# Rearranging the prologue of a one-core attention and expert kernel: load order, engine of the scalings and key copies, place of the statistics, order of the first maxima

## The chip, the cores and the metric

The kernel runs on one core of one Trainium2 chip. The metric is device microseconds of one execution; lower is better. Three runs of the kernel before gave 1066.01, 1066.62 and 1066.67 us, so its time is 1066.62 us. One further execution was profiled; all rows come from it.

## What is computed

One layer: cross attention, then a mixture of experts, both with residuals. Cut to what matters here:

```
l  = layernorm(layernorm(x))               # x: 2048 x 256, "latents"; gains ln_l_g, ln_l_b
c  = layernorm(ctx)                        # ctx: 1601 x 192, "context"; gains ln_x_g, ln_x_b
q  = l @ Wq.T
kv = concat([c @ Wkv.T, l @ Wlkv.T])       # 1601 + 2048 keys and values, 4 heads of 64
attn = softmax(where(mask, rmsnorm(q)*qn_g/8 @ (rmsnorm(k)*kn_g).T, -max))   # mask on the context keys
x  = x + (attn @ v) @ Wo.T + bo
x  = x + top2_of_8_experts(layernorm(x))   # silu(gate)*up, then w2
```

All matrices are float32. The change touches only what comes before the first attention score.

## The kernel before, in words

Each engine has its own instruction stream; semaphores order them. The program has a prologue (the first 140 us), 16 attention units (four query blocks by four heads), and the expert stage. The prologue is the subject.

**Tiles.** Keys lie in 29 tiles of 128: t = 0 to 12 are context (13 tiles, 192 channels), t = 13 to 28 are latents (16 tiles, 256 channels). The prologue is a software pipeline written by hand: in step s each engine runs its function `pro` with work on different tiles, in this order.

- TensorE (L1283): transposes of the normalised tile s into `bX` (L1288); after that the products of tile s-1 for queries and keys into `bA` (L1300), in latent steps the query transposes of an older tile (L1312), the values of tile s-1 into `bV` (L1317); last the four key transposes of tile s-3 into `bK` (L1328). The products of L1300 wait until `knat` of two tiles earlier has been read out of the same bank. L1328 waits until both readers of the previous `bK` are done (semaphores `s2`, `klo`).
- VectorE (L894): multiplies `bX` by the gain and adds the offset, giving `xT` (L902, two instructions); normalises tile s+1 into `xn` (L891); sums squares of tile s-2 (`ss`, L911); writes the low part of the keys of tile s-4 (L916, semaphore `klo`, below called the key rest); reciprocal norms (L923, L926); normalised queries `qn` (L932) and keys `knat` (L937) of tile s-2.
- ScalarE (L633): squares of tile s-2 (L640), the high part of the keys of tile s-4 into `S2` (L646), the values (L651), the scaled queries `QT` (L659), the norms (L665), and the copy of the high keys from `S2` into `S1` (L669).
- GpSimd: zeroes rows 64 to 127 of all of `S2` in one memset (L451), then per tile writes the mask column into `knat` (L459) and adds the output bias to x (L465), which SyncE stores.

**Head of the prologue.** SyncE loads context tiles 0-1, then 2-11, then the last, then x, the latent weights and others. The queue of ScalarE issues the context weights, eight loads of the gains, four of the query and key norm gains, and the mask, whose element (t, p) goes to partition p (L624), one byte per descriptor. VectorE takes the statistics of all 13 context tiles (L867 to L884), normalises tile 0, then waits for the mask (L943), the norm gains and the eight gains (L953), and only then runs step 0.

**x statistics.** After step 6 VectorE takes the statistics of all 16 x tiles in one go (L959 to L962).

**End of the prologue.** VectorE waits for everything, zeroes and fills the lower rows of `Q2` (L983, L984), and makes two small constants. ScalarE copies the first queries (L693, L697), TensorE computes 32 score pieces of 464 keys (`piece`, L1346, query tile by query tile) of which VectorE takes the maxima (L1002). These 32 must be done before the first unit. SyncE waits for all keys and queries (L351 to L353) before it loads the first pieces of expert weights, which ScalarE and GpSimd split (L735, L492); six of them stand in ScalarE's stream before the first unit.

Of the kernel before, what the change touches and what calls it, by code (L numbers as in the profile page):

```python
# [4 lines left out]
F32 = mybir.dt.float32  # L5
# [8 lines left out]
P = 128  # L14
# [9 lines left out]
QB = 4  # L24
# [74 lines left out]
def run_units(body):  # L99
    for b in range(NB):  # L100
        for h in range(H):
            body(Unit(b, h))

# [21 lines left out]
def build(nc, x, ctx_in, mask, ln_x_g, ln_x_b, ln_l_g, ln_l_b, qn_g, kn_g, w_lat, w_ctx, wo_t, bo,  # L125
# [13 lines left out]
    with stack:  # L139
# [122 lines left out]
        m_u8 = sb("m_u8", [P, NC], U8, at=t0)  # L262
# [59 lines left out]
        FIRST_BANKS = M_BANKS + [bS[i][:, k, :] for i in range(2) for k in range(2)]  # L322
# [8 lines left out]
        def _(sp):  # L331
            for n, (lo, hi) in enumerate(CTX_LOADS):
# [4 lines left out]
                .then_inc(sem("ctx_in_l"), 16)  # L337
            sp.dma_start(V[:, NC:NK, :], x.rearrange("(t p) d -> p t d", p=P)).then_inc(sem("x_in"), 16)
# [3 lines left out]
            sp.dma_start(rt[:], router_t.rearrange("(k p) n -> p k n", p=P)).then_inc(sem("c_rt"), 16)  # L342

# [90 lines left out]
        def _(pool):  # L434
# [4 lines left out]
            pool.memset(ident[:], 0.0).then_inc(sem("id0"), 1)  # L439
            pool.memset(ctxt[:, NC - 1, :], 0.0).then_inc(sem("ctx_pad"), 1)  # L440
            pool.memset(mcol[:], 0.0).then_inc(sem("mc0"), 1)
            pool.wait_ge(sem("id0"), 1)
            pool.affine_select(out=ident[:], in_=ident[:], compare_op=ALU.not_equal, fill=1.0, base=0,
                               pattern=[[-1, P]], channel_multiplier=1).then_inc(sem("ident"), 1)
            pool.memset(knat[:, :, :, D:D + 1], -1.0).then_inc(sem("kn0"), 1)

            pool.wait_ge(sem("ident"), 1)
            pool.wait_ge(sem("ctx_pad"), 1)
            pool.wait_ge(sem("mc0"), 1)
            pool.wait_ge(sem("kn0"), 1)  # L450
            pool.memset(S2[D:P, :, :].bitcast(F32), 0.0).then_inc(sem("s20"), 1)  # L451
            pool.wait_ge(sem("s20"), 1)


            def k_mask(t):
                if not (t.i is None and t.off < 2):
                    pool.wait_ge(sem("kT_mm"), t.v - 1)
                pool.wait_ge(sem("mcol"), 1)
                pool.tensor_copy(knat[:, t.par, :, D + 1], mcol[:, bass.ds(t.v, 1)].to_broadcast([P, H]))\  # L459
                    .then_inc(sem("kmask"), 1)  # L460
# [6 lines left out]
            pool.wait_ge(sem("c_bo"), 16)  # L467
            for t in range(NC + 2):
                k_mask(Step(None, t))
                if t == 3:  # L470
                    pool.wait_ge(sem("x_in"), 16)
                if t >= 3:
                    x_bias(t - 3)
            for t in range(NC - 1, NT):
                x_bias(t)
# [19 lines left out]
            def constants():  # L495
# [15 lines left out]
                pool.tensor_copy(row[:], row_i[:]).then_inc(sem("row"), 1)  # L511
                pool.wait_ge(sem("U"), 1)
# [4 lines left out]
                pool.wait_ge(sem("row"), 1)  # L517
# [93 lines left out]
        def _(act):  # L611
            act.dma_start(wc[0:P, 0, :], w_ctx[0:P, :]).then_inc(sem("wc_in"), 16)
            act.dma_start(wc[0:CIN - P, 1, :], w_ctx[P:CIN, :]).then_inc(sem("wc_in2"), 16)
            gains = ((ln_x_g, CIN), (ln_x_b, CIN), (ln_l_g, DIM), (ln_l_b, DIM))
            for n, (g, w) in enumerate(gains):
                for k in range(2):
                    r = min(P, w - k * P)
                    act.dma_start(cols[0:r, 2 * n + k:2 * n + k + 1],
                                  g[k * P:k * P + r].rearrange("(p a) -> p a", a=1)).then_inc(sem("cols"), 16)
            for n, g in enumerate((qn_g, kn_g)):  # L620
                for k in range(2):
                    act.dma_start(gcol[k * D:(k + 1) * D, n:n + 1], g.rearrange("(p a) -> p a", a=1))\
                        .then_inc(sem("gq"), 16)
            act.dma_start(m_u8[:, 0:NC - 1], mask[0:(NC - 1) * P].rearrange("(t p) -> p t", p=P),  # L624
                          allow_slow_non_contiguous=True).then_inc(sem("m_in"), 16)
            act.dma_start(m_u8[0:CTX - (NC - 1) * P, NC - 1:NC],
                          mask[(NC - 1) * P:CTX].rearrange("(p a) -> p a", a=1)).then_inc(sem("m_in"), 16)


            act.wait_ge(sem("bn"), NC)  # L630
            act.activation(sda[:, 0:NC], mvs[:, 0:NC, 1], ACT.Sqrt, bias=eps[:, 0:1]).then_inc(sem("sd_c"), 1)

            def pro(s, b, c, q=0):  # L633
# [8 lines left out]
                kT = bK[0:A, 0, :].rearrange("p (h c) -> p h c", h=H)  # L642
                if c:
                    c_ = s.back(4)
                    act.wait_ge(sem("kT_mm"), c_.v + 1)
                    act.copy(S2[0:A, :, bass.ds(c_.v * P, P)], kT).then_inc(sem("s2"), 1)  # L646
# [20 lines left out]
                if c:  # L667
                    act.wait_ge(sem("s2"), c_.v + 1)
                    act.copy(S1[0:D, :, bass.ds(c_.v * P, P)],  # L669
                             S2[0:D, :, bass.ds(c_.v * P, P)].bitcast(F32)).then_inc(sem("s1"), 1)  # L670

            def lat_sd():
                act.wait_ge(sem("bn"), NK)
                act.activation(sda[:, NC:NK], mvs[:, NC:NK, 1], ACT.Sqrt, bias=eps[:, 0:1]).then_inc(sem("sd_l"), 1)
                act.wait_ge(sem("v2"), 1)
                act.activation(sda[:, NC:NK], va[:, NC:NK], ACT.Sqrt, bias=eps[:, 0:1]).then_inc(sem("sd_l"), 1)

            act.wait_ge(sem("s20"), 1)
# [125 lines left out]

            for k in range(2):
                act.wait_ge(sem(f"xb_st{k}"), 16 * NT // 2)
            q_hi(0, 0, 0)
            q_hi_1(0, 0, 0)
# [46 lines left out]
        def _(dve):  # L855
# [10 lines left out]
            dve.memset(xT[CIN - P:P, :, 1, :], 0.0).then_inc(sem("xT0"), 1)  # L866
# [8 lines left out]

            for n, (lo, hi) in enumerate(CTX_LOADS):
                dve.wait_ge(sem(f"ctx_in{n}"), 16)
                for t in range(lo, hi):
                    stats(ctxt[:, t, :], t)
            dve.wait_ge(sem("ctx_in_l"), 16)  # L880
            stats(ctxt[:, NC - 1, :], NC - 1)
            aggregate(0, NC)
            dve.wait_ge(sem("sd_c"), 1)
            link(dve.reciprocal(rsd[:, 0:NC], sda[:, 0:NC]))  # L884
# [9 lines left out]
            def pro(s, a, ln, b, c):  # L894
                if a:
                    dve.wait_ge(sem("xT_mm"), s.v + 1)
                    if not (s.i is None and s.off < 2):
                        dve.wait_ge(sem("v_mm"), s.v - 1)
                    for k in range(2):
                        r = P if (k == 0 or a == 'l') else CIN - P  # L900
                        g0 = 0 if a == 'c' else 4
                        dve.tensor_scalar(xT[0:r, s.par, k, :], bX[s.par][0:r, 0, k * P:(k + 1) * P],  # L902
                                          cols[0:r, g0 + k:g0 + k + 1], cols[0:r, g0 + 2 + k:g0 + 3 + k],
                                          ALU.mult, ALU.add).then_inc(sem("xT"), 1)
# [36 lines left out]
            apply(Step(None, 0), 'c')  # L941

            dve.wait_ge(sem("m_in"), 32)  # L943
            dve.wait_ge(sem("mc0"), 1)
            NF = NC - 1
            link(dve.tensor_scalar(mcol[:, 0:NF], m_u8[:, 0:NF], -1.0, BIG, ALU.add, ALU.mult))
            link(dve.memset(mcol[:, NF:NC], -BIG))
            dve.tensor_scalar(mcol[0:CTX - NF * P, NF:NC], m_u8[0:CTX - NF * P, NF:NC], -1.0, BIG, ALU.add, ALU.mult)\
                .then_inc(sem("mcol"), 1)
            dve.wait_ge(sem("gq"), 64)  # L950
            dve.scalar_tensor_tensor(gT[:], gcol[:, 0:1], SCALE, gcol[:, 1:2], ALU.mult, ALU.mult)\
                .then_inc(sem("gs"), 1)
            dve.wait_ge(sem("cols"), 128)  # L953
            dve.wait_ge(sem("xT0"), 1)
            run_steps(dve, 0, 2, lambda s: pro(s, 'c', 'c', 0, 0))
            run_steps(dve, 2, 4, lambda s: pro(s, 'c', 'c', 'c', 0))
            run_steps(dve, 4, LAT_AT + 1, lambda s: pro(s, 'c', 'c', 'c', 1))

            dve.wait_ge(sem("x_in"), 16)  # L959
            for t in range(NT):  # L960
                stats(V[:, NC + t, :], NC + t)
            aggregate(NC, NK)  # L962
            run_steps(dve, LAT_AT + 1, LAT_AT + 2, lambda s: pro(s, 'c', 'c', 'c', 1))
            L = slice(NC, NK)
            dve.wait_ge(sem("sd_l"), 1)
            link(dve.reciprocal(rsd[:, L], sda[:, L]))
# [313 lines left out]
        def _(pe):  # L1280
# [65 lines left out]
            def piece(v, h, k, banks):  # L1346

                i, g = divmod(k, NG)
                if k == 0:
                    pe.wait_ge(sem("q2"), v + 1)  # L1350
# [305 lines left out]
```

## Time and profile before

| | |
|---|---|
| median of 3 runs | 1066.62 us |
| profiled execution | 1064.43 us |
| its span, first to last instruction | 1062.7 us |
| busy over the span | TensorE 91%, VectorE 67%, GpSimd 54%, ScalarE 46% |
| mean granted TensorE clock | 0.971 |

The chain that ended last is 70% TensorE and 7% VectorE of the span. In the page's 40 slices (26.6 us each) TensorE reads 2, 6, 9, 9, 8, 6 tenths in the first six and 9 nearly everywhere after; VectorE reads 3, 8, 8, 8, 8, 6 there. A row of the timeline gives start, duration, engine, line, operation, output and inputs, the count of merged instructions, and in brackets the idle time before it with what ended it.

### The profile page before, as it was taken

The page shows a single profiled execution, that of the slowest core. Times are in us where ns is not written, and L with a number is a line of the kernel's source. Part 1 is how long each engine was busy: PE and PEld are TensorE (multiplying, and loading weights), DVE is VectorE, ACT ScalarE, POOL GpSimd, SP SyncE. Part 2 cuts the span into 40 slices and gives each one's busy share as a digit, 9 for nine tenths or more (in the row PEclk, how much of TensorE's full clock was granted, in tenths as well). Part 3 has the DMA queues.
Part 4 walks back from the last instruction along what each step waited for, and adds up shares of the span by engine and source line. Part 5 has one row for each costly group of instructions (what it writes and reads, how often), then busy time and mean ns, then how long its engine had stood idle before and what let it go on. Part 6 is the DMA issues. An engine that isn't in the chain of part 4 may idle for free.

```text
span 1062.7 us, 15497 instructions
## 1 busy us (share of the span) xinstructions
PE 965.9 (91%) x4570; PEld 629.9 (59%) x4571; DVE 710.6 (67%) x1412; ACT 484.5 (46%) x752; POOL 570.1 (54%) x439
## 2 busy tenths in 40 slices
PE   2699869999999999999999999999996869999994
PEld 1565535556555556556656556565554658888883
DVE  3888886776786776776776776767787424444442
ACT  0456625545555455555555655654552213233231
POOL 5130016776677676776676676676700235565552
PEclk9899978999999999999999999999998889999998
DMA  6010021121122121221122121221338673333331
GB/s 185 20 46 15 0 94 54 52 74 60 60 67 68 65 74 61 74 71 60 65 80 65 60 85 55 70 75 60 131 142 338 235 295 52 53 52 52 53 51 24
DMA packets 70627, 87.51 MB, mean 82 GB/s; under 512 B 12619, under 2 KB 66828, under 8 KB 68524
## 3 DMA queue, kind: packets, MB, share of 16 engines
q1 hardware_dynamic: 52046, 70.73, 19.0%
q0 software_dynamic: 7488, 10.39, 6.0%
q10 hardware_dynamic: 11038, 5.71, 1.9%
q8 instruction: 28, 0.46, 0.2%
q14 instruction: 27, 0.22, 0.1%
HBM read 50.03 MB, written 36.77 MB: 82 GB/s over the span
## 4 chain that ended last, share of the span: by engine, by line
PE 70%; DVE 7%; issue 4%; DMA 3%; ACT 2%; ACTq 0%; POOL 0%; POOLq 0%; DVEq 0%
PE bPV L1433 20%; PE bM L1353 10%; PE bS L1422 9%; PE bS L1423 8%; DVE mpart L1002 2%; DMA out<-ysb,sidx 2%; PE bG L1543 2%; PE bY L1543 2%; PE bY L1544 2%; PE bY L1545 2%; PE bH L1560 2%; PE bT L1368 2%; ACT PT L780 2%; PE bG L1545 1%; PE bG L1544 1%
## 5 line engine op out<-in xcount | busy, mean ns | idle before, releaser
L1002 DVE TENSOR_REDUCE mpart<-bM 128x1 f32<-128x464 f32 x492 | 295.7, 635 | 126.5 <-PE bM L1353 125.1
L488 POOL TENSOR_TENSOR acc_p<-acc_p,PT 128x1024 f32<-128x1024 f32 x120 | 302.3, 2519 | 104.1 <-ACT PT L780 100.5
L780 ACT ACTIVATE PT<-bS 128x1024 f32<-128x1024 f32 (+1 forms) x240 | 237.6, 997 | 202.0 <-PE bS L1423 173.1
L1433 PE MATMUL bPV<-PT,V 128*64 128x512 f32 x928 | 230.6, 604 | 0.0
L1422 PE MATMUL bS<-QQ,S 128*128 128x512 f32 x464 | 189.8, 409 | 3.2 <-ACT PT L780 0.8
L1353 PE MATMUL bM<-S,QQ 128*128 128x464 f32 x492 | 174.2, 413 | 11.8 <-DVE mpart L1002 6.4
L1423 PE MATMUL bS<-QQ,S 128*128 128x512 f32 x464 | 183.7, 396 | 0.0
L1353 PEld LDWEIGHTS bM<-S,QQ 128*128 128x128 f32 x492 | 84.7, 191 | 95.1 <-DVE mpart L1002 70.3
L492 POOL TENSOR_TENSOR wraw<-wraw,whi 128x256 fp32r<-128x256 f32 x96 | 85.3, 889 | 69.3 <-ACT whi L735 69.3
L1433 PEld LDWEIGHTS bPV<-PT,V 128*64 128x64 f32 x928 | 58.7, 136 | 104.5 <-issue 91.8
L1422 PEld LDWEIGHTS bS<-QQ,S 128*128 128x128 f32 x464 | 87.8, 189 | 55.0 <-issue 26.0
L1423 PEld LDWEIGHTS bS<-QQ,S 128*128 128x128 f32 x464 | 87.9, 189 | 14.2
L1034 DVE TENSOR_TENSOR acc_d<-acc_d,PT 128x1024 f32<-128x1024 f32 (+1 forms) x58 | 89.0, 1535 | 0.8
L488 POOL TENSOR_TENSOR acc_p<-PT 128x1024 f32<-128x1024 f32 x15 | 38.3, 2556 | 86.5 <-ACT PT L780 86.5
L735 ACT CAST whi<-wraw 128x256 fp32r<-128x256 f32 x96 | 38.5, 402 | 78.9 <-DMA wraw<-w 78.5
L595 POOL DMA_INDIRECT out<-ysb,ring_s x34 | 54.3, 1597 | 37.0 <-POOL ring_s L588 30.4
L1254 DVE TENSOR_TENSOR hs<-hs,bU 128x512 f32<-128x512 f32 x39 | 26.8, 688 | 62.5 <-PE bU L1545 62.5
L836 ACT CAST hTe<-bH 128x512 fp32r<-128x512 f32 x39 | 22.9, 587 | 69.5 <-PE bH L1560 69.5
L1543 PE MATMUL bY<-W,hTe 128*128 x156 | 48.2, 309 | 1.5 <-DVE hTe L1248 1.5
L571 POOL DMA_INDIRECT xg<-xln_d,ring_g x34 | 34.4, 1012 | 27.0 <-POOL ring_g L567 27.0
L1544 PE MATMUL bY<-W,hTe 128*128 x156 | 45.0, 288 | 0.0
L1545 PE MATMUL bY<-W,hTe 128*128 x156 | 44.9, 288 | 0.0
(244 smaller groups left out, 1437.9 us busy)
## 6 DMA issues: line engine op xcount, KB each, us to landing
W<-wsp_d SPq DMA_DIRECT2D x16, 1536.0 KB, 11.7
wraw<-w SPq DMA_DIRECT2D x96, 128.0 KB, 2.4
wsp_d<-whi SPq DMA_DIRECT2D x96, 128.0 KB, 2.4
wsp_d<-wraw SPq DMA_DIRECT2D x96, 128.0 KB, 1.7
V<-x SPq DMA_DIRECT2D x1, 2048.0 KB, 12.6
xb_d<-xbs SPq DMA_DIRECT2D x16, 128.0 KB, 1.7
x<-xb_d ACTq DMA_DIRECT2D x12, 128.0 KB, 2.0
out<-x ACTq DMA_DIRECT2D x12, 128.0 KB, 1.7
```

Of the source, the lines that this page charges most:

```text
L488: pool.tensor_tensor(acc_p[:], one, PT[:, q % NPT, :, :], ALU.add).then_inc(sem("z_p"), 1)
L492: pool.tensor_tensor(wraw[:, n % 2, :].bitcast(F32R), wraw[:, n % 2, :], whi[:, n % 2, :].bitcast(F32), ALU.subtract).then_inc(sem("wsplit ...
L780: act.activation(PT[:, p % NPT, 0:n, :], bS[(w.h + p) % 2][:, 0:n, :], ACT.Exp).then_inc(sem("exp"), 1)
L1002: dve.tensor_reduce(mpart[:, i, g:g + 1], banks[k % len(banks)][:, 0:PIECE], AX, ALU.max)\
L1034: dve.tensor_tensor(acc_d[:, 0:m, :], one, PT[:, q % NPT, 0:m, :], ALU.add).then_inc(sem("z_d"), 1)
L1353: pe.matmul(banks[k % len(banks)][:, 0:PIECE], Q2[:, h % 2, i * P:(i + 1) * P], S2[:, h, g * PIECE:(g + 1) * PIECE], start=True, stop=True ...
L1422: pe.matmul(bS[sl][:, b, :], S1[:, h, c * P:(c + 1) * P], Q1[:, h % 2, :], start=True, stop=False)
L1423: last = pe.matmul(bS[sl][:, b, :], S2[:, h, c * P:(c + 1) * P], Q2[:, h % 2, :], start=False, stop=True)
L1433: last = pe.matmul(bPV[b * D:(b + 1) * D, 0, :], V[:, c, h * D:(h + 1) * D], PT[:, p % NPT, b, :], start=c < 2, stop=c >= NK - 2, skip_gro ...
L1543: pe.matmul(out_ap, st_hi, w[:, s, 0, lo:lo + n], start=first, stop=False)
L1544: pe.matmul(out_ap, st_lo, w[:, s, 0, lo:lo + n], start=False, stop=False)
L1545: return pe.matmul(out_ap, st_hi, w[:, s, 1, lo:lo + n], start=False, stop=last_)
```

## The change

- SyncE loads context tiles 0-3 first, then 4-11; the mask is loaded by rows (13 rows of 128 bytes) on SyncE's queue, in front of x; the latent gains and the query and key norm gains move to the end of SyncE's list of loads.
- GpSimd turns the mask into float, TensorE transposes it, VectorE makes the mask column from that.
- VectorE takes statistics of tiles 0-3 and starts; those of tiles 4-12 come after tiles 0 to 2 are normalised.
- The scalings (`xT`) run on ScalarE as Identity with scale and bias columns.
- The copy of the high keys into `S1` runs on GpSimd, which also zeroes `S2` by tile.
- The x statistics are spread over steps 4 to 8 (3, 3, 3, 3, 4), their aggregation is in step 9.
- `Q2`'s lower rows are set by GpSimd; ScalarE copies the first queries two steps earlier; the first 32 pieces go by age of the keys, and use the score banks first.

```diff
+def place(v, k):
+    return (k % QB, k // QB) if v == 0 else divmod(k, NG)
...
-        FIRST_BANKS = M_BANKS + [bS[i][:, k, :] for i in range(2) for k in range(2)]
+        FIRST_BANKS = [bS[i][:, k, :] for i in range(2) for k in range(2)] + M_BANKS
...
+            sp.wait_ge(sem("mc0"), 2)
+            sp.dma_start(m_u8[0:NC - 1, :], mask[0:(NC - 1) * P].rearrange("(t p) -> t p", p=P)).then_inc(sem("m_in"), 16)
...
-            pool.memset(S2[D:P, :, :].bitcast(F32), 0.0).then_inc(sem("s20"), 1)
+            def rest_zero(lo, hi):
+                pool.memset(S2[D:P, :, lo * P:hi * P].bitcast(F32), 0.0).then_inc(sem("s20"), 1)
+            def keys_hi(t):
+                pool.wait_ge(sem("s2"), t + 1)
+                pool.tensor_copy(S1[0:D, :, t * P:(t + 1) * P], S2[0:D, :, t * P:(t + 1) * P].bitcast(F32))\
+                    .then_inc(sem("s1"), 1)
...
+            rest_zero(0, 4)
+            pool.wait_ge(sem("m_in"), 32)
+            pool.tensor_copy(mrow[0:NC, :], m_u8[0:NC, :]).then_inc(sem("mcol"), 1)
+            for t in range(NK + 2):
+                if t < NC + 2:
+                    k_mask(t)
+                if t + 4 < NK:
+                    rest_zero(t + 4, t + 5)
+                if 3 <= t < 3 + NT:
+                    x_bias(t - 3)
+                if t >= 2:
+                    keys_hi(t - 2)
+            pool.wait_ge(sem("v_mm"), NK)
+            pool.memset(Q2[D:P, :, :].bitcast(F32), 0.0).then_inc(sem("q20"), 1)
+            pool.memset(Q2[D:D + 2, :, :].bitcast(F32), 1.0).then_inc(sem("q20"), 1)
...
             def pro(s, a, b, c, q=0):        # ScalarE
+                if a:
+                    act.wait_ge(sem("xT_mm"), s.v + 1)
+                    for k in range(2):
+                        act.activation(xT[0:r, s.par, k, :], bX[s.par][0:r, 0, k * P:(k + 1) * P], ACT.Identity,
+                                       scale=cols[0:r, g0 + k:g0 + k + 1], bias=cols[0:r, g0 + 2 + k:g0 + 3 + k])
                 if b:   # squares, as before
                 if c:   # S2, as before, and a wait for rest_zero
                 ...
-                if c:
-                    act.copy(S1[0:D, ...], S2[0:D, ...].bitcast(F32)).then_inc(sem("s1"), 1)
...
+            for t in range(4, NC - 1):       # VectorE
+                pro(Step(None, t), 'c', 'c', 1)
+                for _ in range(X_STATS.get(t, 0)):
+                    stats(V[:, NC + done, :], NC + done)
+                if t == X_AGGR_AT:
+                    aggregate(NC, NK)
...
+            pe.wait_ge(sem("mcol"), 1)
+            pe.transpose(bK[:, 0, 0:NC], mrow[0:NC, :], ident[0:NC, 0:NC]).then_inc(sem("mcol"), 1)
...
+            pe.wait_ge(sem("q20"), 2)
+            pe.wait_ge(sem("sq"), NK)
+            pe.wait_ge(sem("q_n"), NT)
+            pe.wait_ge(sem("knat"), NK)
+            for k in range(NM):
+                if k == len(FIRST_BANKS) - len(M_BANKS):
+                    pe.wait_ge(sem("v_cp"), NK)
+                    pe.wait_ge(sem("qT"), NT)
+                piece(0, 0, k, FIRST_BANKS)
...
-CTX_LOADS = ((0, 2), (2, NC - 1))
-LAT_AT = 6
+CTX_LOADS = ((0, 4), (4, NC - 1))
+X_STATS = {4: 3, 5: 3, 6: 3, 7: 3, 8: 4}
+X_AGGR_AT, X_SD_AT = 9, 10
```

## Rows read from the trace of the kernel before

**Rows 1.** Busy time in one stretch: PE, PEld, DVE, ACT, POOL, clock, DMA, GB/s.

```profile
39.40:48.80 9.40, 3.15 (x15) 2.33 (x15) 9.27 (x42) 1.78 (x5) 0.87 (x2) 0.82 0.04 14
```

**Rows 2.** Timeline of TensorE: the transposes of tiles 3, 13 and 28.

```profile
26.83 0.38 PE L1288 MATMUL bX<-ident,xn 128*128 128x128 f32 x2
...
65.77 0.38 PE L1288 MATMUL bX<-ident,xn 128*128 128x128 f32 x2
...
122.19 0.38 PE L1288 MATMUL bX<-ident,xn 128*128 128x128 f32 x2
```

**Rows 3.** Timeline of the first 22 us, all engines.

```profile
1.79 12.47 POOL L451 MEMSET S<- 64x14848 f32 x1
...
3.04 1.22 ACTq L618 DMA_DIRECT2D cols<-ln_x_b  x2
...
19.32 0.17 DVE L946 TENSOR_SCALAR mcol<-m_u 128x12 f32<-128x12 uint8 x1 [2.73 <-DMA m_u<-mask]
...
19.79 0.71 DVE L902 TENSOR_SCALAR xT<-bX,cols 128x128 f32<-128x128 f32 x2
...
21.39 1.91 PE L1300 MATMUL bA<-wc,xT 128*128 128x256 f32 x4
```

**Rows 4.** DMA issues by line, first 30 us: KB each, median us to landing.

```profile
cols<-ln_x_b ACTq DMA_DIRECT2D x1, 0.2 KB, 6.1
```

**Rows 5.** Timeline of one context step, from the transposes of tile 10.

```profile
56.35 0.38 PE L1288 MATMUL bX<-ident,xn 128*128 128x128 f32 x2
...
56.73 0.73 POOL L465 TENSOR_TENSOR xbs<-V,bob 128x256 f32<-128x256 f32 x1
...
56.86 0.72 DVE L902 TENSOR_SCALAR xT<-bX,cols 128x128 f32<-128x128 f32 x2 [0.22 <-PE bX L1288]
...
58.23 0.69 DVE L916 TENSOR_TENSOR S<-bK,S 64x512 f32 x1
...
59.07 0.60 PE L1328 MATMUL bK<-ident,knat 128*66 128x128 f32 x4 [0.32 <-DVE S L916]
...
59.56 0.43 PE L1288 MATMUL bX<-ident,xn 128*128 128x128 f32 x2
```

**Rows 6.** Timeline of one latent step, from the transposes of tile 22.

```profile
99.22 0.38 PE L1288 MATMUL bX<-ident,xn 128*128 128x128 f32 x2
...
100.69 0.69 DVE L911 TENSOR_REDUCE ss<-bSq 128x8 f32<-128x512 f32 x1
...
103.00 0.41 DVE L937 TENSOR_TENSOR knat<-bA,rn 128x256 f32<-128x256 f32 x1
...
103.56 1.95 PE L1300 MATMUL bA<-wl,xT 128*128 128x512 f32 x4 [0.37 <-DVE knat L937]
```

**Rows 7.** Groups by line and shape, first 160 us: busy us, mean ns, idle before.

```profile
L646 ACT CAST S<-bK 66x512 fp32r<-66x512 f32 x11 | 6.4, 581 | 5.3 <-PE bK L1328 5.3
...
L869 DVE BATCH_NORM_STATS2 st<-V 128x6 f32<-128x256 f32 x16 | 5.3, 409 | 0.0
...
L640 ACT ACTIVATE bSq<-bA 128x256 f32<-128x256 f32 x13 | 4.7, 364 | 7.5 <-PE bA L1300 7.5
...
L665 ACT ACTIVATE nrm<-ss 128x4 f32<-128x4 f32 x13 | 2.7, 205 | 17.4 <-DVE ss L911 17.4
...
L659 ACT ACTIVATE QT<-bV,gT 128x256 f32<-128x256 f32 x4 | 1.9, 474 | 0.0
...
L631 ACT ACTIVATE sda<-mvs,eps 128x13 f32<-128x13 f32 x1 | 0.3, 306 | 0.0
```

**Rows 8.** Timeline of the prologue's end, all engines.

```profile
133.79 0.58 ACT L646 CAST S<-bK 66x512 fp32r<-66x512 f32 x1 [0.62 <-PE bK L1328]
...
135.72 0.81 SPq L363 DMA_DIRECT2D wraw<-w  x2
...
139.01 1.11 PE L1353 MATMUL bM<-S,QQ 128*128 128x464 f32 x2 [5.03 <-ACT QQ L693]
...
140.11 1.17 DVE L1002 TENSOR_REDUCE mpart<-bM 128x1 f32<-128x464 f32 x2
```

More of the change, by code:

```diff
@@ L874, in aggregate, with spread @@
                     dve.bn_aggr(mvs[:, t, :], st6[:, t, :]).then_inc(sem("bn"), 1)
[L876 to L882, printed above, removed]
+            def spread(lo, hi):
+                link(dve.reciprocal(rsd[:, lo:hi], sda[:, lo:hi]))
+            lo, hi = CTX_LOADS[0]
+            dve.wait_ge(sem("ctx_in0"), 16)
+            for t in range(lo, hi):
+                stats(ctxt[:, t, :], t)
+            aggregate(lo, hi)
             dve.wait_ge(sem("sd_c"), 1)
-            link(dve.reciprocal(rsd[:, 0:NC], sda[:, 0:NC]))
+            spread(lo, hi)
             def apply(t, kind):
@@ L892, in apply, with pro @@
                                   ALU.subtract, ALU.mult).then_inc(sem("ln"), 1)
[L894 to L904, printed above, removed]
+            def pro(s, ln, b, c):
                 if ln:
@@ L941, in _ @@
             apply(Step(None, 0), 'c')
-            dve.wait_ge(sem("m_in"), 32)
-            dve.wait_ge(sem("mc0"), 1)
+            for t in range(2):
+                pro(Step(None, t), 'c', 0, 0)
+            dve.wait_ge(sem("ctx_in1"), 16)
+            dve.wait_ge(sem("ctx_in_l"), 16)
+            for t in range(hi, NC):
+                stats(ctxt[:, t, :], t)
+            aggregate(hi, NC)
+            dve.wait_ge(sem("sd_c"), 2)
+            spread(hi, NC)
+            pro(Step(None, 2), 'c', 'c', 0)
@@ L959, in _ @@
[L959 to L963, printed above, removed]
-            L = slice(NC, NK)
-            dve.wait_ge(sem("sd_l"), 1)
-            link(dve.reciprocal(rsd[:, L], sda[:, L]))
-            link(dve.tensor_tensor(va[:, L], rsd[:, L], rsd[:, L], ALU.mult))
-            dve.tensor_tensor(va[:, L], va[:, L], mvs[:, L, 1], ALU.mult).then_inc(sem("v2"), 1)
@@ L999, in piece @@
             def piece(v, k, banks):
-                i, g = divmod(k, NG)
+                i, g = place(v, k)
                 dve.wait_ge(sem("m_mm"), NM * v + k + 1)
@@ L1174, in _ @@
             maxima(0)
+            for q in range(2):
+                dve.tensor_copy(twin[q * D:(q + 1) * D, :], ident[q * D:(q + 1) * D, q * D:(q + 1) * D])\
+                    .then_inc(sem("twin"), 1)
+            dve.memset(onec[:], 1.0).then_inc(sem("twin"), 1)
             run_units(unit)
```

204 lines of the change are left out of this document (106 added, 98 removed).

## The prediction

> **What bounds the kernel now.** I read the chain of waits first: it is mostly TensorE from the first attention unit on, and nothing there is edited. So I looked at the stretch before it. The timeline of the first 22 us shows that VectorE stands until 19.32 us for the mask to land, although tile 0 has been normalised; the first scaling starts at 19.79 us and the first product at 21.39 us [rows 3]. From there I follow the pipeline by the transposes of each tile: tile 3 at 26.83, tile 13 at 65.77, tile 28 at 122.19 us [rows 2], so 38.94 us for ten context steps and 56.42 us for fifteen steps that end with the latents. The ten contain one hole: from 39.4 to 48.8 us TensorE is busy 3.15 of 9.40 us and VectorE 9.27, at a granted clock of 0.82 [rows 1]; that is the 16 x statistics in one go. Elsewhere a context step takes 59.56 - 56.35 = 3.21 us, and the row before its end says what held TensorE: the key rest on VectorE [rows 5]. The latent steps take (122.19 - 99.22)/6 = 3.83 us on average [rows 2, 6], and there the product of L1300 was held by `knat`, also on VectorE [rows 6]. The end runs from 122.19 to the first maximum at 140.11 us: 17.92 us [rows 2, 8].
>
> The sum is made in the profiled execution's time: span 1062.7 us, execution 1064.43 us, and the median of the runs is 1066.62 us, 2.2 us above. The edits lie in the first 140 us, so I take the difference off the median.
>
> **1. The head.** Gone from the path: the byte-wise mask, four of the eight gain loads, the norm gains, and the statistics of nine tiles. What ends last now? The statistics of four tiles can start when 384 KB have landed; I put that at 5 us, four statistics and aggregations at 1.5 us, the root, the reciprocal and tile 0 at 1.2 us: ready by 8 us, its transposes by 8.5. The two columns `ln_x_b` are issued at 3.04 to 4.26 us, so the last at about 3.7, and land 6.1 us after issue [rows 3, 4]: 9.8 us. These are issued at the same place in the new kernel, so I keep 9.8 (bounds: 8.5 if the slot is limited by the statistics; 13 if more traffic lies in front of them). ScalarE then scales tile 0 in 0.9 us, and the first product starts at 10.9 us instead of 21.39. TensorE's first products run slow, 1.91 us for four [rows 3], and will again. The mask's 13 rows follow the context loads on their queue; they are needed only by the key transposes of tile 0, some 8 us after the first product, so I cost the cast, the transpose and three small VectorE operations at nothing; if the rows landed after 18 us, each microsecond would show. Gain **10.4 us** (bounds 6.5 to 12).
>
> **2. One scaling on ScalarE.** No row has both a scale column and a bias column. Rows without a column: 364 ns for 256 elements, 205 ns for 4 [rows 7], so about 270 for 128. One column adds 100 to 110 ns: `QT` 474 against 364, `sda` 306 against 205 [rows 7]. So two columns give 270 + 210 = 480 ns; bounds 270 (nothing added) and 580. Consecutive ScalarE operations overlap by about 100 ns in this timeline, so a pair takes 0.76 us of the engine. VectorE's pair took 0.72 [rows 5]. The Trainium skill (ScalarE: Activation LUTs, "What ACT_TABLE_LOAD costs") has 186 ns + 0.833 ns per element, 93 ns more for each column operand and 93 ns of overlap; an estimate by it is 479 ns each and the same 0.76 us, which no row here shows for this form.
>
> **3. Context steps.** VectorE loses 0.72 us a step, ScalarE swaps the `S1` copy for a pair of scalings. But what counts is the chain that closes the loop on `bK`. New order on ScalarE: scalings, squares, `S2`. Hence from the transposes: 0.51 to the start of scaling [rows 5], 0.76 the pair, 0.27 the squares (364 less overlap), 0.58 `S2` [rows 7], 0.03, the key rest 0.69, 0.15 to the key transposes, 0.49 to the next transposes [rows 5]. Sum 3.48; where key transposes start back to back it is 0.04 less, so I use **3.45 us** against 3.21 (3.06 in the best steps). In the kernel before `S2` ran beside VectorE's scaling; now they are in series on one engine. Bounds: 3.03 with the cheap scaling, 3.65 with the dear one. VectorE has room for the statistics: 5.3 us / 16 = 0.33 each [rows 7], so 1.0 us in a step of which it uses 2.2 us of 3.45; for the step with four and for the aggregation I add 0.5 us in all. Ten steps: 34.5 + 0.5 = 35.0 against 38.94. Gain **3.9 us**. If the spread statistics weren't covered, it would be 6.5 us of VectorE work more, and the gain gone.
>
> **4. Latent steps.** Before: the sum of squares starts 1.47 us after the transposes (99.22 to 100.69), `knat` ends at 103.41, 4.19 after them, and the held product starts 0.15 later [rows 6]. The product of the next step can't start before 4.34, and from its start to the following transposes is a fixed piece c. Two steps take 4.34 + c = 7.66, so c = 3.32. After: the squares (0.58 for 512 elements, like `S2` [rows 7]) begin only behind the scalings, at 0.51 + 0.76 = 1.27, end at 1.85, and the sum starts at 1.88, 0.41 later than now; everything behind it on VectorE follows in the same order, so `knat` ends at 4.60. A step is (4.60 + 0.15 + 3.32)/2 = **4.03 us** against 3.83. Twelve of these, and 3.45 + 3.5 + 3.8 for the three in which latents enter: 59.1 against 56.42. Loss **2.7 us** (bounds: 0 with the cheap scaling; 4 with the dear one).
>
> **5. GpSimd.** Per step: mask column 0.2, a zeroing 12.47/29 = 0.43 [rows 3], bias 0.73 [rows 5], key copy of 512 elements. Its bounds: 0.43 (as a memset) and 1.46 (twice the bias add of 256 elements [rows 5]); I take 0.7, nearer the memset since it reads one tensor. With waits 2.4 us a step, at worst 3.2, both under 3.45, and nobody waits for `S1` before the end. So nothing in the steps.
>
> **6. The end.** ScalarE's two query copies (0.62 each) now stand in front of the last two `S2`, and the last products come 0.8 us later behind their transposes than before, as `knat` does. The last `S2`, which began 133.79 - 122.19 = 11.60 us after tile 28's transposes [rows 2, 8], begins at 12.7 and ends at 13.3. Then GpSimd: the last key copy, 14.05; only then, in its stream, the two memsets of `Q2`, 0.86 us each for 1024 elements (12.47 x 1024/14848 [rows 3]), 15.95. TensorE's first piece waits for them. It takes 0.55 (1.11 for two [rows 8]), and the first maximum starts at 16.6 us instead of 17.92. Gain **1.3 us** (bounds -0.5 with the dear copy, 4 if nothing held the memsets). The order by key age lets pieces start before the last keys, but the memsets come after the last `S2` anyway, so I give it nothing. The 32 maxima keep their pace on VectorE. The weight loads start 0.7 us later behind tile 28 than before (135.72 [rows 8]); with their six rounds they end shortly before the maxima.
>
> Sum: 10.4 + 3.9 - 2.7 + 1.3 = 12.9 us, so **1053.7 us**.
>
> **The rivals.** *A, the chain is as I say*: 1053.7. The `knat` and key-rest releasers speak for it; chance 0.57.
>
> *B, scaling is cheap* (about 0.29 us each, 0.4 less a pair, or overlapped with the squares): context steps 3.05, latent steps 3.83 as now; 10.4 + (38.94 - 31.0) + 0 + 1.3 = 19.6, so 1047.0. Against it: both column rows show an extra 100 ns. Chance 0.22.
>
> *C, the head opens late*: the gain columns or the mask rows land 4 us later than I think, because the larger first context load and the mask are in front of or beside them. 12.9 - 4.5: 1058. Chance 0.09.
>
> *D, given back at the end*: the weight split or the memsets on GpSimd hold the first unit 5 us or so. 1058 to 1060. Chance 0.07.
>
> *E, slower*: GpSimd's memset and copies (0.43 + 0.7, up to 1.9 us a step that weren't there) stretch VectorE's key rest and `knat` or block them. It decides from 12.9/25 = 0.5 us a step; at 0.7 us it costs 17.5, so 1071. Against it: VectorE's pair of 0.72 us ran right under a GpSimd add of 0.73 us [rows 5] and was no longer than elsewhere. Chance 0.03. The Trainium skill (GPSIMD Engine Reference, "Key points") says that GpSimd shares its SBUF interfaces with VectorE and names contention with VectorE operations that have two SBUF inputs or run in a two-port mode; the trace has no GpSimd copy in the prologue to test that with, and the key rest has one PSUM input.
>
> *F, no change* (the steps lengthen by all that the head wins): 0.02.
>
> **How the numbers follow.** A measurement of this kernel tells 0.2% (2.1 us) from no change. Faster: A, B, C and nearly all of D, 0.93; within: 0.03; slower: 0.04. The range 1045 to 1060.5 covers A with its bounds, B, C and most of D.
>
> **What would show it.** First product at about 11 us; scalings on ScalarE of 480 ns; context steps of 3.45 us held by the key rest, no hole near 40 us and the clock at 1.00 there; latent steps of 4.0 us held by `knat`; first piece held by GpSimd's `Q2` memset; first maximum near 126.6 us. Wrong: steps of 3.1 us (B), a wait for a DMA before 15 us (C), TensorE idle in front of the first unit behind the weight split (D), key rest above 0.9 us (E).

## The result and the profile after

Four runs of the changed kernel gave 1052.95 to 1056.56 us, median 1053.64 us, against 1066.32 us for the kernel before in the same comparison: ratio 0.9886, 95% interval 0.9867 to 0.9905. The same kernel in a later comparison (e0_changed, below) gave 1054.57 us, ratio 0.9887, interval 0.9871 to 0.9903. The profiled execution took 1052.95 us, its span 1051.1 us, 11.6 us less than before.

Read the span by the same marks as before. First the timeline of the head of the changed kernel, all engines.

```profile
5.08 1.14 DVE L912 BATCH_NORM_STATS2 st<-ctxt 128x6 f32<-128x192 f32 x4 [3.23 <-DMA ctxt<-ctx_in]
...
7.60 1.23 PE L1325 MATMUL bX<-ident,xn 128*128 128x128 f32 x4 [7.60 <-DVE xn L935]
...
9.30 0.28 POOL L494 CAST mrow<-m_u 13x128 f32<-13x128 uint8 x1 [5.56 <-DMA m_u<-mask]
...
10.47 1.49 ACT L672 ACTIVATE xT<-bX,cols 128x128 f32<-128x128 f32 x4 [3.65 <-DMA cols<-ln_x_b]
...
11.32 2.07 PE L1337 MATMUL bA<-wc,xT 128*128 128x256 f32 x4 [2.50 <-ACT xT L672]
```

Tiles 0 and 1 are transposed at 7.6 us and the mask is there at 9.3; ScalarE stands 3.65 us for the last gain load. The first product starts at 11.32 us, at 21.39 before [rows 3]. Next TensorE's timeline of the changed kernel, the transposes of tiles 3, 13 and 28.

```profile
16.81 0.44 PE L1325 MATMUL bX<-ident,xn 128*128 128x128 f32 x2
...
51.92 0.38 PE L1325 MATMUL bX<-ident,xn 128*128 128x128 f32 x2
...
111.25 0.38 PE L1325 MATMUL bX<-ident,xn 128*128 128x128 f32 x2
```

| | before | after | gain, us | predicted |
|---|---|---|---|---|
| to tile 3 | 26.83 | 16.81 | 10.0 | 10.4 |
| tile 3 to 13 | 38.94 | 35.11 | 3.8 | 3.9 |
| tile 13 to 28 | 56.42 | 59.33 | -2.9 | -2.7 |
| tile 28 to first maximum | 17.92 | 17.11 | 0.8 | 1.3 |
| sum | 140.11 | 128.36 | 11.75 | 12.9 |

Behind the first maximum both profiles take the same time within 0.2 us: 1062.7 - 140.11 = 922.6 and 1051.1 - 128.36 = 922.7. The medians differ by 12.7 us, the two profiled executions by 11.5.

The hole near 40 us [rows 1] is gone. Busy time and clock of the changed kernel in the stretch from tile 3 to 13 (columns as in rows 1):

```profile
16.80:51.90 35.10, 27.66 (x141) 20.16 (x141) 30.91 (x103) 20.03 (x61) 19.13 (x39) 1.00 0.11 33
```

The granted clock is 1.00, the upper of its two levels (2.4 GHz); VectorE is still busy 31 of 35 us, and not only with what I had thought. Groups of the changed kernel by line and shape, first 150 us:

```profile
L672 ACT ACTIVATE xT<-bX,cols 128x128 f32<-128x128 f32 x45 | 18.8, 454 | 44.6 <-PE bX L1325 41.0 <-DMA cols<-ln_x_b 3.6
...
L485 POOL CAST S<-S 64x512 fp32r<-64x512 f32 x29 | 17.5, 603 | 46.3 <-ACT S L687 46.2
...
L945 DVE TENSOR_REDUCE ss<-bSq 128x8 f32<-128x512 f32 x16 | 11.0, 690 | 12.2 <-ACT bSq L681 12.2
...
L935 DVE TENSOR_SCALAR xn<-ctxt,mvs,rsd 128x192 f32<-128x192 f32 x13 | 7.0, 549 | 0.6 <-PE bX L1325 0.6
```

A scaling takes 454 ns with its two columns, where 480 was worked out. VectorE now waits 12.2 us in all for the squares of latent tiles: that is the series of ScalarE. And `xn` takes 549 ns on average, 366 before, though nothing about it was edited. The timeline of one context step with statistics shows where.

```profile
26.97 0.38 PE L1325 MATMUL bX<-ident,xn 128*128 128x128 f32 x2
27.18 1.07 DVE L912 BATCH_NORM_STATS2 st<-V 128x6 f32<-128x256 f32 x3
...
27.39 0.80 ACT L672 ACTIVATE xT<-bX,cols 128x128 f32<-128x128 f32 x2 [1.48 <-PE bX L1325]
...
28.09 0.37 ACT L681 ACTIVATE bSq<-bA 128x256 f32<-128x256 f32 x1
28.11 0.73 POOL L480 TENSOR_TENSOR xbs<-V,bob 128x256 f32<-128x256 f32 x1
...
28.16 0.79 DVE L935 TENSOR_SCALAR xn<-ctxt,mvs,rsd 128x192 f32<-128x192 f32 x1
...
28.39 0.58 ACT L687 CAST S<-bK 66x512 fp32r<-66x512 f32 x1
...
28.87 0.41 DVE L945 TENSOR_REDUCE ss<-bSq 128x4 f32<-128x256 f32 x1
...
29.32 0.69 DVE L950 TENSOR_TENSOR S<-bK,S 64x512 fp32r<-64x512 f32 x1
```

`S2` ends at 28.97, but the key rest starts at 29.32: VectorE itself is late, by the statistics and by an `xn` of 0.79 us that ends 0.11 us after a GpSimd add (28.84). Then one latent step of the changed kernel.

```profile
86.76 0.38 PE L1325 MATMUL bX<-ident,xn 128*128 128x128 f32 x2
...
87.26 0.81 ACT L672 ACTIVATE xT<-bX,cols 128x128 f32<-128x128 f32 x2 [1.43 <-PE bX L1325]
...
87.96 0.59 ACT L681 ACTIVATE bSq<-bA 128x512 f32<-128x512 f32 x1
...
88.58 0.69 DVE L945 TENSOR_REDUCE ss<-bSq 128x8 f32<-128x512 f32 x1 [0.57 <-ACT bSq L681]
...
89.85 0.52 POOL L468 MEMSET S<- 64x512 f32 x1
...
90.03 0.37 DVE L957 TENSOR_SCALAR rn<-nrm 128x8 f32<-128x8 f32 x1
...
91.01 0.41 DVE L971 TENSOR_TENSOR knat<-bA,rn 128x256 f32<-128x256 f32 x1
...
91.58 1.95 PE L1337 MATMUL bA<-wl,xT 128*128 128x512 f32 x4 [0.18 <-DVE knat L971]
```

This is the chain of the prediction: scalings, squares, sum, `knat`, product. The sum starts 1.82 us after the transposes (1.88 predicted, 1.47 before [rows 6]) and `knat` ends 4.66 after them (4.60 predicted). The end of the prologue:

```profile
124.19 0.58 ACT L687 CAST S<-bK 66x512 fp32r<-66x512 f32 x1 [1.37 <-PE bK L1365]
...
124.90 0.61 POOL L485 CAST S<-S 64x512 fp32r<-64x512 f32 x1 [1.72 <-ACT S L687]
...
125.57 0.95 POOL L512 MEMSET QQ<- 64x1024 f32 x1
...
126.57 0.94 POOL L514 MEMSET QQ<- 2x1024 f32 x1
127.57 1.27 PEld L1394 LDWEIGHTS bS<-S,QQ 128*128 128x128 f32 x4 [3.39 <-POOL QQ L514]
...
128.36 1.74 DVE L1034 TENSOR_REDUCE mpart<-bS 128x1 f32<-128x464 f32 x3 [2.16 <-PE bS L1394]
```

The first piece is held by GpSimd's memsets behind the last key copy, as predicted. The last `S2` starts 12.9 us after tile 28 (12.7 predicted), a memset takes 0.95 us (0.86), and the first piece takes 0.79 us (127.57 to 128.36, at a granted clock of 0.50) where 0.55 was worked out.

### The profile page after: what moved, and what is told of

Read it like the earlier page. It is cut to its first block, busy times and chain, and to the rows that moved or that the text cites. A ratio compares the mean times of both kernels' runs of the same rounds, so it can differ in the third digit from the quotient of the medians.

```text
span 1051.1 us, 15535 instructions
## 1 busy us (share of the span) xinstructions
PE 965.6 (92%) x4571; PEld 628.7 (60%) x4572; DVE 695.0 (66%) x1353; ACT 488.5 (46%) x782; POOL 593.6 (56%) x497
## 3 DMA queue, kind: packets, MB, share of 16 engines
q1 hardware_dynamic: 52968, 70.73, 19.3%
## 4 chain that ended last, share of the span: by engine, by line
PE 73%; DVE 10%; DMA 5%; issue 5%; ACT 4%; POOL 1%; ACTq 1%; DVEq 0%; POOLq 0%
PE bPV L1478 20%; PE bM L1394 10%; PE bS L1467 9%; PE bS L1468 8%; DVE mpart L1034 2%; PE bA L1337 2%; DMA out<-ysb,sidx 2%; ACT PT L817 2%; PE bG L1588 2%; PE bY L1588 2%; PE bT L1409 2%; PE bY L1589 2%; PE bY L1590 2%; PE bH L1605 1%; PE bG L1590 1%
## 6 DMA issues: line engine op xcount, KB each, us to landing
V<-x SPq DMA_DIRECT2D x1, 2048.0 KB, 11.5
```

## The experiments

All are edits of the changed kernel. "Tiles 3 to 13" and the like are differences of the transposes' starts in each profile. The kernel before ran beside every experiment and took 1065.5 to 1066.5 us. The 95% interval of a ratio to it is about 0.2% (2 us) wide to either side, so a difference of medians below that isn't shown by the medians; there the stretches of the profiles must decide.

**e2_order: ScalarE's step in another order.**

```diff
             def pro(s, a, b, c, q=0):    # ScalarE
-                if a: ...   # the two scalings
                 if b: ...   # squares
                 if c: ...   # S2
+                if a: ...   # the two scalings
                 if b: ...   # values
```

> The changed kernel with ScalarE's step in another order: squares, S2, then the scalings (now: scalings, squares, S2). Nothing is added or left out. Theory (the series scalings, squares, S2, sum of squares, knat is the step's length): with squares and S2 done while TensorE still works on the step before, context steps without statistics fall from 3.33 to 2.9 us, those with statistics from 3.6 to about 3.3 (VectorE's load), latent steps from 4.08 to 3.6 to 3.7 (TensorE's load). Tiles 3 to 13: 31.5 us, 13 to 28: 54, so about 9 us faster than the changed kernel: 1044.5. Rival (ScalarE's order is covered, TensorE or VectorE load sets the step): 1053.6.

Measured 1044.17 us (1042.2 to 1044.66), ratio to before 0.9796 (0.9778 to 0.9814). Tiles 3 to 13: 32.62 us, 13 to 28: 51.98 (3.47 a step). The order alone is worth 9.5 us; the rival is out. From tile 22 to 28 TensorE is now busy 21.45 of 21.49 us, 22.18 of 24.49 in the changed kernel: it sets the latent step itself. One detail missed: the five steps with statistics stayed at 3.62 us on average instead of 3.3. One of them:

```profile
26.26 0.58 ACT L677 CAST S<-bK 66x512 fp32r<-66x512 f32 x1 [0.99 <-PE bK L1365]
26.27 1.07 DVE L912 BATCH_NORM_STATS2 st<-V 128x6 f32<-128x256 f32 x3
...
26.74 0.80 ACT L686 ACTIVATE xT<-bX,cols 128x128 f32<-128x128 f32 x2
...
27.20 0.72 POOL L480 TENSOR_TENSOR xbs<-V,bob 128x256 f32<-128x256 f32 x1
27.25 0.79 DVE L935 TENSOR_SCALAR xn<-ctxt,mvs,rsd 128x192 f32<-128x192 f32 x1
```

ScalarE is early, VectorE is full, and `xn` is again 0.42 us too long beside the GpSimd add.

**e3_plain_copy: scalings as plain copies** (gain and offset of both first normalisations left out).

```diff
-                        act.activation(xT[0:r, s.par, k, :], bX[...], ACT.Identity, scale=cols[...], bias=cols[...])
+                        act.copy(xT[0:r, s.par, k, :], bX[s.par][0:r, 0, k * P:(k + 1) * P])
```

> The changed kernel with the scalings as plain copies on ScalarE, without scale and bias columns: gain and offset of both first normalisations are left out. It prices the two column operands. Theory: a copy takes about 0.27 us instead of 0.45, the pair saves 0.3 us of the series; a context step saves 0.3 where no statistics are, a latent step half of it, 0.15: about 4 to 5 us in all, 1049. Rival (column operands cost nothing on this path): same 0.45 us and 1053.6.

Measured 1049.18 us (1048.82 to 1049.51). Tiles 3 to 13: 33.6, 13 to 28: 56.3 us, against 35.1 and 59.3. A scaling without its columns took 268 ns, 454 with them, so the column operands stand on the path; had they been free, the time would have been 1049.2, some 2 us above case B of the prediction (1047.0).

**e1_scale_on_dve: scalings back on VectorE.**

```diff
-            def pro(s, ln, b, c):        # VectorE
+            def pro(s, a, ln, b, c):
+                if a: ...   # dve.tensor_scalar twice, as in the kernel before; ScalarE's are removed
```

> The changed kernel with one part undone: the scalings are back on VectorE, in front of its other work of the step. Theory (the loop that closes on the key banks, not the load of an engine, sets the step): S2 runs beside the scaling again, so latent steps go from 4.08 back to about 3.83 us (tiles 13 to 28: 56.4 against 59.3), while the x statistics, 0.33 us each, are no longer covered (tiles 3 to 13: 38.5 against 35.1). Sum within 1 us of the changed kernel, 1054. Rival (moving 0.72 us a step off the busiest engine is what wins): about 0.7 x 25 = 17 us slower, 1070.

Measured 1057.41 us (1056.98 to 1057.53), 3.8 above the changed kernel. Tiles 3 to 13: 37.76 (+2.65), 13 to 28: 57.75 (-1.58), tile 3 at 18.52 (+1.7, VectorE now also waits for the gains). The signs are those of the theory and the rival's 17 us are out. The sizes missed: 1054 was expected, and tiles 13 to 28 should have fallen to 56.4. `xn` of latent tiles took 674 ns on average there against 428, again beside GpSimd work; that this is what made the difference, no run isolates. Of the 1.7 us at tile 3 part may be the scatter of the last section.

**e5_stats_block: x statistics in one go.**

```diff
-X_STATS = {4: 3, 5: 3, 6: 3, 7: 3, 8: 4}
-X_AGGR_AT, X_SD_AT = 9, 10
+X_STATS = {6: 16}
+X_AGGR_AT, X_SD_AT = 6, 7
```

> The changed kernel with one part undone: all 16 x statistics and their aggregation in one go after step 6. Theory (VectorE has about 1 us of room in a step, so spreading hides part of them): the five steps with statistics fall from 3.6 to 3.33 us (1.4 us won), and one step takes 5.6 to 6 us more: tiles 3 to 13 take 35.1 - 1.4 + 5.8 = 39.5 us, about 4.4 us slower than the changed kernel, 1058. Rival (the hole was only moved, VectorE does the same work): 1053.6.

Measured 1059.44 us (1058.95 to 1060.8). Tiles 3 to 13 took 39.47 us, as worked out, so the spreading is worth 4.4 us. In this profile another 1.9 us are in the head, where tile 3 came at 18.75; the changed kernel's own second profile has 18.31 (see the last section), so the edit needn't be their cause.

**e6_head_wait: all context statistics before tile 0.**

```diff
+            # moved here: wait for ctx_in1 and ctx_in_l, statistics, aggregate, root and reciprocal of tiles 4 to 12
             apply(Step(None, 0), 'c')
             for t in range(2):
                 pro(Step(None, t), 'c', 0, 0)
```

> The changed kernel with one part undone: VectorE takes the statistics of all 13 context tiles before it normalises tile 0; mask by rows and the short list of gain loads stay. Theory (the head opens when the later of gains, 10.4 us, and tile 0 comes): tile 0 is ready at 13.0 instead of 7.5, the first product starts at 14.3 to 14.6 us instead of 11.32, and all behind it shifts: 3.2 us slower, 1056.8, so the mask and the shorter list hold the other 7 us of the head's gain. Rival (loading in pieces is the whole gain): first product near 21 us, 1063.

Measured 1058.67 us (1057.28 to 1059.95). First product at 14.59 us, as worked out; the rival's 21 us are out. Tile 3 came at 21.57, 4.8 us later than in the first profile of the changed kernel (16.81) and 3.3 later than in its second (18.31). The total is 1.9 us above the 1056.8 expected, and this scatter of TensorE's first products (last section) can be the reason.

**e11_mask_bytes: a byte-wise mask load to wait for** (loaded besides the rows, used only as a wait).

```diff
+            act.dma_start(m_old[:, 0:NC - 1], mask[0:(NC - 1) * P].rearrange("(t p) -> p t", p=P),
+                          allow_slow_non_contiguous=True).then_inc(sem("m_old"), 16)
...
             act.wait_ge(sem("cols"), 64)
+            act.wait_ge(sem("m_old"), 16)
```

> The changed kernel with a part of the old head put back: the mask is loaded a second time by bytes on ScalarE's queue, behind the short list of gains, and ScalarE waits for it before the first scaling (the mask column is still made from the rows). Theory (the byte-wise load holds the queue for 4.5 us and lands 5 us after that): it lands near 13.7 us, the first product starts at 14.6 instead of 11.3 and all is 3.3 us later, 1057; with the long list of twelve gain loads in front it was 19.3. Rival (small loads land when the traffic of the big ones allows): lands near 11, no more than 1 us slower, 1054.5.

Measured 1062.12 us (1058.58 to 1063.73), and both expectations are wrong in size. The timeline:

```profile
4.42 0.63 ACTq L661 DMA_DIRECT2D m_old<-mask  x1
...
17.08 1.49 ACT L676 ACTIVATE xT<-bX,cols 128x128 f32<-128x128 f32 x4 [10.07 <-DMA m_old<-mask]
```

It holds the queue for 0.63 us only, but lands 12.7 us after its issue; the gain loads just ahead of it landed 7 us after theirs. The first product starts at 17.93. So the byte-wise mask alone, even behind the short list, costs 6.6 of the 10.1 us that the first product had won. In the kernel before, the same load was issued at 9.16 us and landed at 19.3, so issuing it 4.7 us earlier brought its landing forward by only 2.2 us. In both, the 16 DMA engines were nearly always busy (97% of the first 18 us before, 100% of the first 17 here); how much of the 12.7 us is this load's own transfer and how much waiting behind other traffic, no run separates.

The 4.5 us of the expectation belonged to another load. These rows are from the timeline of the kernel before:

```profile
9.80 4.47 ACTq L626 DMA_DIRECT2D m_u<-mask  x1
...
15.59 0.31 ACT L631 ACTIVATE sda<-mvs,eps 128x13 f32<-128x13 f32 x1
```

L626 loads the mask of the last, partial tile; the byte-wise load of the other twelve (L624) held the queue 0.60 us there too. Behind L626 stood ScalarE's table load and root, so tile 0 was normalised at 16.2 us although its statistics were aggregated by 12.0. The mask, landing at 19.3, hid this.

**e8_gains_first: gain loads ahead of the context weights.**

```diff
-            act.dma_start(wc[0:P, 0, :], ...)        # and the second one
             for n, g in enumerate((ln_x_g, ln_x_b)): ...
+            act.dma_start(wc[0:P, 0, :], ...)        # and the second one
```

> The changed kernel with the four gain loads ahead of the two loads of the context weights on ScalarE's queue. Theory (the first scaling is held by the last gain load, whose slot in the queue counts): the gains are issued 1.1 us earlier and meet less traffic, so they land at 8 to 9.3 instead of 10.4 us; the weights land at about 10. First product at 9.6 to 10.3 us, 1 to 1.7 us faster than the changed kernel, 1052.3. Rival (the landing is set by the traffic of the context tiles, not by the slot): 10.4 us as now, 1053.6.

Measured 1055.87 us (1054.03 to 1056.37), ratio 0.9898 (0.9875 to 0.9920). That isn't the gain expected; whether it is slower than the changed kernel (0.9886, 0.9867 to 0.9905) the medians don't show. The timeline of its head:

```profile
8.91 0.80 ACT L672 ACTIVATE xT<-bX,cols 128x128 f32<-128x128 f32 x2 [1.70 <-DMA cols<-ln_x_b]
...
11.84 0.66 PE L1325 MATMUL bX<-ident,xn 128*128 128x128 f32 x2 [3.20 <-DMA wc<-w_ctx]
...
12.29 1.91 PE L1337 MATMUL bA<-wc,xT 128*128 128x256 f32 x4
```

The gains landed 1.6 us earlier, as I said; the weights landed at 11.8, and TensorE's wait for them stands in front of the transposes of tile 1. The first product starts at 12.29 us, 11.32 and 11.64 in the two profiles of the changed kernel: one wait was turned into another, 0.7 to 1.0 us later.

**e4_q2_early: the memsets of `Q2` two tiles earlier in GpSimd's stream.**

```diff
             for t in range(NK + 2):
...
+                if t == NK:
+                    pool.wait_ge(sem("v_mm"), NK)
+                    ...   # the two memsets of Q2, with their waits
                 if t >= 2:
                     keys_hi(t - 2)
...
-            ...   # the same two memsets behind the loop
```

> The changed kernel with GpSimd's two memsets of Q2 in front of its copies of the keys of tiles 27 and 28, as soon as the last product has read the memory under Q2. Theory (the first score piece is held by these memsets behind the last key copy, 127.57 us): the first maximum starts at 126.2 us instead of 128.36, right behind the last key rest and the query rest on VectorE: 2.1 us faster, 1051.5. Rival (the six rounds of the weight split stand in front of the first unit): no gain, 1053.6.

Measured 1052.74 us (1052.31 to 1053.43). From tile 28 to the first maximum 15.06 us instead of 17.11: the 2.05 us are there and the rival is out, but this profile's tile 3 came 0.7 us later, and the medians' 0.9 us is within their noise.

**e7_bias_late: e2_order with the bias adds seven steps later.**

```diff
-                if 3 <= t < 3 + NT:
-                    x_bias(t - 3)
+                if 10 <= t < 10 + NT:
+                    x_bias(t - 10)
...
```

> The kernel with ScalarE's other order (e2_order), and GpSimd's 16 bias adds seven steps later, behind the steps with statistics. In those steps normalising a tile took 0.79 us on VectorE where it takes 0.37, each time while a bias add ran on GpSimd. Theory (the two hold each other up when both read the state buffer): without the adds it takes 0.37 to 0.45 us, the steps with statistics, which in e2_order are all VectorE, fall from 3.6 to 3.2 us, 2 us faster than e2_order: 1042. It may come back in the latent steps, where the adds now lie (TensorE sets the step there, 3.6 us, so I expect no more than 1 us). Rival (the long xn is the statistics' own after-effect): 0.79 stays, 1044.2.

Measured 1046.01 us (1045.77 to 1046.6), ratio 0.9810 (0.9790 to 0.9830) against 0.9796 (0.9778 to 0.9814) for e2_order: not the 2 us gained, and a loss isn't shown by the medians. Tiles 3 to 13: 31.92 (-0.7), 13 to 28: 53.57 (+1.6). A step with statistics:

```profile
26.76 0.60 POOL L485 CAST S<-S 64x512 fp32r<-64x512 f32 x1
26.83 0.65 DVE L935 TENSOR_SCALAR xn<-ctxt,mvs,rsd 128x192 f32<-128x192 f32 x1
```

With the add gone, GpSimd's key copy slid under `xn`, which ends 0.12 us after that copy. And in the latent steps `rn` of eight columns took 431 ns on average, 240 in e2_order. The collision moved; the rival (an after-effect of the statistics) is out, since the length follows the GpSimd operation.

**e9_order_q2: e2_order and e4_q2_early together; e0_changed: the changed kernel beside it.**

> Both edits that gained: ScalarE's order (squares, S2, scalings) and GpSimd's early memsets of Q2. Theory (the two lie in different stretches and add): tiles 3 to 13 in 32.6 us, 13 to 28 in 52 us as in e2_order, and the first maximum 14.5 to 15 us after the transposes of tile 28 instead of 16.0: 1 to 1.5 us under e2_order, 1043, and 10.5 us under the changed kernel. Rival (with the steps shorter, the copies of queries or the last S2 set the end and the early memsets win nothing): 1044.2.

> The changed kernel itself once more, as the partner of the two kernels below in the same comparison: 1053.6 us.

e9_order_q2: 1041.82 us (1039.63 to 1043.58), ratio to before 0.9777 (0.9763 to 0.9790). e0_changed in the same comparison: 1054.57, 0.9887 (0.9871 to 0.9903). The intervals are far apart: this version is 12.8 us faster than the changed kernel and 24.7 faster than the one before. Tiles 32.62 and 51.98 as in e2_order; from tile 28 to the first maximum 14.18 us against 16.00. Its end:

```profile
110.06 0.95 POOL L510 MEMSET QQ<- 64x1024 f32 x1
...
111.06 0.94 POOL L512 MEMSET QQ<- 2x1024 f32 x1
...
114.99 0.68 DVE L1029 TENSOR_TENSOR QQ<-QT,QQ 64x512 fp32r<-64x512 f32 x1
...
115.60 2.27 DVE L1035 TENSOR_REDUCE mpart<-bS 128x1 f32<-128x464 f32 x4
```

**e10_zero_once: e9_order_q2 with one memset of `S2` at the start.**

```diff
-            rest_zero(0, 4)
+            rest_zero(0, NK)
...
-                if t + 4 < NK:
-                    rest_zero(t + 4, t + 5)
...
```

> e9_order_q2 with GpSimd zeroing the lower rows of S2 in one memset at the start (12.5 us, as in the kernel before) instead of tile by tile. Theory (a GpSimd operation holds up a VectorE operation that reads the state buffer alone, and the reverse; each pass of such a pair costs up to 0.4 us where VectorE sets the step): 25 memsets of 0.52 us leave the steps, VectorE's rn goes from 0.24 to 0.17 to 0.20 us, but the bias add moves to where xn stands or away from it by chance; the mask cast waits until 14.4 us, which is still ahead of its reader at 16.6. So 0 to 2 us faster than e9_order_q2, 1042. Rival (memsets write only and disturb nothing): the same as e9_order_q2 within 0.5 us.

Measured 1046.06 us (1045.0 to 1046.83), 4.2 slower than e9_order_q2, where 0 to 2 faster was expected. The steps did as I said: tiles 3 to 13 in 31.29 us (-1.3), 13 to 28 in 51.18 (-0.8). The first four steps with statistics fell from 3.63 to 3.21 us on average, and `xn` in them from 0.79 (once 0.76) to 0.36: without the memset the bias add comes earlier, and `xn` starts only as it ends. The timeline of one:

```profile
27.48 0.73 POOL L480 TENSOR_TENSOR xbs<-V,bob 128x256 f32<-128x256 f32 x1
...
28.15 0.36 DVE L933 TENSOR_SCALAR xn<-ctxt,mvs,rsd 128x192 f32<-128x192 f32 x1
```

The head is what I had not seen. Its timeline:

```profile
1.93 12.47 POOL L468 MEMSET S<- 64x14848 f32 x1
...
7.24 7.62 DVE L933 TENSOR_SCALAR xn<-ctxt,mvs,rsd 128x192 f32<-128x192 f32 x2
...
14.66 1.09 PE L1323 MATMUL bX<-ident,xn 128*128 128x128 f32 x4 [14.66 <-DVE xn L933]
```

The two `xn`, 0.67 us together in the changed kernel, started at 7.24 and ended at 14.86, 0.46 us after GpSimd's memset (14.40). The statistics and the reciprocal ran under the same memset undisturbed (reciprocal done at 7.2). So a memset does disturb: the rival is out as well. No run joins the short steps of this version with the head of e9_order_q2.

## Why the prediction was right

**Head, 10.4 against 10.0 us.** The step was: the last gain load sets the first scaling. It does; it landed at 10.45 us, 0.6 later than worked out. That the size came out so near is partly luck: in e0_changed, the same kernel, the gain at tile 3 was 8.5 us. e11 shows that the byte-wise mask alone would hold the first product to 17.9 us, e6 that the early statistics are worth 3.3 us there. What shorter lists of gains on ScalarE's queue are worth by themselves, no run shows. I costed the tile-by-tile zeroing of `S2` at nothing. That is true of it, but not of the single memset that it replaces: e10 shows that with it VectorE could not have normalised tile 0 before 14.4 us, and about 5 us of the gain would have been lost (tile 3 came at 21.89 us there, at 16.82 in e9_order_q2). The kernel before never met this, since its `xn` came at 16 us.

**Scaling, 480 against 454 ns.** Right, with both column prices read off other groups [rows 7]. The pair holds ScalarE 0.70 us up to the squares (27.39 to 28.09), not 0.76. e3 confirms that it is on the path.

**Context steps, 35.0 against 35.11 us: right by luck, two errors that cancel.** The four steps without statistics took 3.30 us on average, 0.15 less than 3.45, which would make 1.5 us in ten; the six with statistics or their aggregation took 3.65, 2.1 us more in all where 0.5 was added. The step that failed is "VectorE has room for the statistics": it had 1.25 us of room for 1.0 us of them, but not also for `xn` at 0.79 instead of 0.37 us. e10 shows it against e9_order_q2: with `xn` back at 0.36, the first four steps with statistics lost the same 0.42 us. What I took as evidence against case E, a scaling with a PSUM source beside a GpSimd add [rows 5], told nothing of an operation whose source is in the state buffer. So a part of case E was real, but in `xn` and `rn`, not in the key rest and `knat` that it named (0.68 and 0.42 us as before), and at some 0.4 us in a few steps, not 0.7 in all.

**Latent steps, 4.03 against 4.08 us** (tiles 22 to 28, 24.49/6). The chain was right link by link; `rn` of eight columns beside GpSimd's memset (298 ns on average, 184 before) makes up the rest. e2 is the proof: nothing but the order on ScalarE was edited, and the steps fell to 3.6, TensorE's own length. The order was an open choice that the prediction priced as a loss of 2.7 us and didn't question.

**GpSimd, key copy 0.7 against 0.60 us**; the memset of one tile 0.52, not 0.43.

**End, 1.3 against 0.8 us.** Held as predicted by the `Q2` memsets; these took 0.95 us each, the last key copy came 0.2 us later and the first piece took 0.2 us longer. e4 shows the full 2.05 us behind them.

The total, 1053.7 predicted and 1053.64 measured, is closer than its parts, and that closeness is luck: the parts sum to 11.75 us in the profile against 12.9 predicted, the medians of the runs happen to differ by 12.7, and the same kernel measured again gave 1054.57. No run undoes the order of the first pieces by age of the keys, which the prediction gave nothing.

## What to carry to other kernels

Moving work off the busiest engine is worth what it does to the loop that closes on a buffer, not what it takes off the engine's total: here the move of the scalings won 3.8 us (partly in the head, where runs scatter), their place in ScalarE's stream 9.5 more. In a pipeline written by hand, try letting an engine first do what frees the others' banks and only then what waits for this step's input. A long GpSimd memset at the start is not free because nobody waits for its result: look at which VectorE operations run under it.

## What the hardware showed that was not expected

VectorE operations that read one float32 tensor from the state buffer and write there (`xn`, `rn`) didn't end before the GpSimd operation that had started ahead of them, in all the rows read here. `xn` ended 0.11 us after a bias add (0.79 us instead of 0.37) and 0.12 after a key copy (0.65); two of them ended 0.46 us after the 12.47 us memset (7.6 us for both, 0.67 without it); `rn` ended 0.03 us after a 0.52 us memset (0.37 instead of 0.18). Statistics, reductions, reciprocals and operations with a PSUM source kept their durations beside the same GpSimd work (statistics of 256 elements 411 ns against 409, the key rest 684 in both kernels). The Trainium skill (GPSIMD Engine Reference, "Key points") names contention with VectorE operations in a two-port mode or with two SBUF inputs; the trace agrees if `xn` and `rn`, which read one tensor, run in such a mode, which no run here shows directly. The size of the stall is the runs' own.

TensorE's first products are slow for a time that varies from run to run: four take 1.91 to 2.07 us, later ones 1.03 to 1.10, though the granted clock reads 1.00 throughout; no run here shows the cause. In the first profile of the changed kernel the products of tile 1 at 14.82 us were already fast, in e0_changed those at 15.63 still took 1.72, and tile 3 came at 18.31 instead of 16.81. Over runs of this one kernel the time spread from 1052.95 to 1056.56 us, so a gain under 2 us in the head can't be read off one run.
